# Attention and experts on one core: the tables' writes and constant rows move to ScalarE's queue, and each bf16 part is stored once and repeated by the loads

## The reference

```
q, k, v = split_heads(x @ Wq + bq), split_heads(x @ Wk + bk), split_heads(x @ Wv + bv)
scores = einsum('bhqd,bhkd->bhqk', q, k) / scale
pos_k = (rel_embeddings @ Wk + bk)                      # 128 buckets per head
c2p = take_along_axis(einsum('bhqd,hpd->bhqp', q, pos_k), c2p_pos)
p2c = take_along_axis(einsum('bhkd,hpd->bhkp', k, pos_k), p2c_pos)
scores = scores + (c2p + swapaxes(p2c)) / scale
ctx = einsum('bhqk,bhkd->bhqd', softmax(scores), v)
```

## Time and profile before

| | us |
|---|---|
| median of 3 runs (2073.40 to 2077.61) | 2073.94 |
| the profiled execution | 2074.24 |
| its span, first to last instruction | 2072.4 |
| outside the span | 1.8 |
| PE busy | 1716.4 (83%) |
| DVE busy | 1358.2 (66%) |
| ACT busy | 1071.2 (52%) |
| POOL busy | 1071.1 (52%) |
| DMA moved | 465.95 MB, mean 225 GB/s |
| SP's queue, share of the 16 engines' time | 64.7% |
| ACT's queue, the same | 3.3% |

### The profile page before, as it was taken

How to read it: one execution, slowest core, us unless ns; L and a number is a source line. 1 busy time by engine, 2 the same in 40 slices (tenths; PEclk the granted TensorE clock), 3 DMA queues, 4 the chain that set the end, 5 groups by cost and what they waited for, 6 DMA issues and landing times. The chain is left out here.

```text
span 2072.4 us, 40517 instructions
## 1 busy us (share of the span) xinstructions
PE 1716.4 (83%) x13688; PEld 1153.3 (56%) x13688; DVE 1358.2 (66%) x3937; ACT 1071.2 (52%) x2169; POOL 1071.1 (52%) x1265
## 2 busy tenths in 40 slices
PE   1981159999989899999999999999993566799997
PEld 1440035555555555555555555655552455799996
DVE  1662058789888788888788887888872464243333
ACT  1662136666667566666666666666661461122221
POOL 0210067677766667667576676766740450233332
PEclk9996569999999999999999999999996575899999
DMA  3697378777777877777877777777736961677772
GB/s 117 190 303 245 108 241 265 246 261 251 244 254 257 253 251 245 258 251 259 254 250 257 250 261 248 251 257 254 240 105 154 289 208 36 227 213 221 217 221 81
DMA packets 327354, 465.95 MB, mean 225 GB/s; under 512 B 35516, under 2 KB 260687, under 8 KB 327054
## 3 DMA queue, kind: packets, MB, share of 16 engines
q1 hardware_dynamic: 314814, 428.09, 64.7%
q10 hardware_dynamic: 7344, 20.84, 3.3%
q0 software_dynamic: 4992, 14.43, 1.9%
HBM read 269.90 MB, written 193.65 MB: 224 GB/s over the span
## 5 line engine op out<-in xcount | busy, mean ns | idle before, releaser
L864 ACT ACTIVATE t_probsT<-t_flip 128x512 f32<-128x512 f32 x1024 | 611.5, 607 | 245.2 <-PE t_flip L762 128.0
L816 DVE TENSOR_REDUCE t_most<-t_scores 128x1 f32<-128x640 f32 (+1 forms) x512 | 437.2, 854 | 263.9 <-PE t_scores L739 257.9
L858 ACT COPY t_table<-t_table_ps 128x512 f32<-128x512 f32 x512 | 299.2, 584 | 227.7 <-DMA skew_d<-t_table 138.2
L835 DVE TENSOR_SCALAR t_band<-t_band,t_top 128x384 f32<-128x384 f32 (+1 forms) x512 | 367.6, 718 | 0.0
L912 POOL TENSOR_TENSOR t_near<-t_near,t_masks 128x384 f32<-128x384 f32 (+1 forms) x128 | 147.2, 1150 | 371.6 <-DMA t_near<-skew_d 370.9
L776 PE MATMUL t_sum_ps<-t_probsT,t_vals 128*32 128x256 f32 x4096 | 330.9, 395 | 0.2 <-ACT t_probsT L864 0.2
L718 PE MATMUL t_table_ps<-t_rows,t_quest 96*128 96x256 bf16 x512 | 144.8, 283 | 176.3 <-ACT t_table L858 89.6
L928 POOL TENSOR_TENSOR t_near<-t_near,t_masks 128x768 f32<-128x768 f32 (+1 forms) x128 | 273.1, 2134 | 0.0
L762 PE MATMUL t_flip<-t_masks,t_band 128*128 128x128 f32 x1408 | 262.2, 275 | 0.0
L820 DVE CUSTOM_DVE_ANT_0 t_band<-t_scores,t_near 128x384 f32<-128x384 f32 (+1 forms) x512 | 262.1, 512 | 0.0
L732 PE MATMUL t_scores<-t_after,t_quest 105*128 105x256 bf16 (+3 forms) x1024 | 246.7, 291 | 0.0
(11 more groups left out here) (181 smaller groups left out, 2373.7 us busy)
## 6 DMA issues: line engine op xcount, KB each, us to landing
skew_d<-t_table SPq DMA_DIRECT2D x128, 1024.0 KB, 9.0
t_near<-skew_d SPq DMA_DIRECT2D x128, 640.0 KB, 6.0
t_near<-skew_d SPq DMA_DIRECT2D x128, 384.0 KB, 4.9
e_w<-in_L_ffn_W_dram ACTq DMA_DIRECT2D x39, 512.0 KB, 4.2
e_w<-in_L_ffn_W_dram SPq DMA_DIRECT2D x39, 512.0 KB, 4.0
split_d<-p_part SPq DMA_DIRECT2D x32, 384.0 KB
t_after<-split_d SPq DMA_DIRECT2D x64, 192.0 KB
t_quest<-split_d SPq DMA_DIRECT2D x64, 192.0 KB
```

Source lines behind the costliest of these rows:

```text
L816: nc.vector.tensor_reduce(most[:, c, 1:2], out[:, wide:S], AX.X, ALU.max)
L835: nc.vector.tensor_scalar(band[n % 2][:, t, 0:wide], band[n % 2][:, t, 0:wide], top[n % 2][:, t:t + 1], None, ALU.subtract).then_inc(level ...
L858: nc.scalar.copy(table[:, h, :, u % 4, :], table_ps[:, :, :]).then_inc(table_kept, 1)
L864: nc.scalar.activation(probsT[s % 3][:, half * 512:(half + 1) * 512], flip_ps[half][:, :], ACT.Exp, scale=SCALE).then_inc(expd, 1)
```

## The change

It does four things.

1. `split_d` becomes `[2, N, PARTS, DH, S]`: for each unit and side three parts of 16 rows. `project` stores each part once, again with 12 DMAs a group, each of 128 rows of 1 KB; the DRAM side has levels 8 (heads), 16 (rows), 512 elements, where it was 128 rows outermost.
2. `load_unit` makes the six slots as it loads, with seven DMAs in place of three, in a new order of slots (the slot tables `QSLOTS`, `KSLOTS` and the pick matrices follow it). Six of the seven have an outermost count of 2 on their DRAM side, four of these with a stride of 0 (the repeat). With the far rows there are 10 DMAs a unit (`HATS`), and the same 288 rows of 2 KB land.
3. `skew_write` moves from SP to ScalarE's queue, behind `exponent(back, 1)` of each fourth step.
4. The constant rows (the ones and minus ones) lie next to each other now, so 18 DMAs set them instead of 42. ScalarE issues them at the start of `attend`, from three tiles that DVE and POOL fill. SP begins with `rows`, then unit 0, then `masks`. PE waits for the constants of a buffer when it first scores with it, no longer for all of them at the start.

The core of the diff:

```
-        split_d = dram("split_d", [2, TERMS, N * DH, S], BF16)
+        split_d = dram("split_d", [2, N, PARTS, DH, S], BF16)
...
                     for m in range(4):
-                        for n, (first, step, many) in enumerate((QSLOTS, KSLOTS)[m // 2]):
-                            at = ((m // 2 * TERMS + first) * (N * DH) + b * D + m % 2 * P) * S + half * G
-                            sp.dma_start(view(split_d, at, [[S, P], [step * N * DH * S, many], [1, G]]),
-                                         part[g % 2][:, n, m, :].unsqueeze(1).to_broadcast([P, many, G])
+                        for n in range(PARTS):
+                            slot = QORDER[n] if m // 2 == 0 else n
+                            at = ((m // 2 * N + b * H + m % 2 * 8) * PARTS + slot) * DH * S + half * G
+                            sp.dma_start(view(split_d, at, [[PARTS * DH * S, 8], [S, DH], [1, G]]), part[g % 2][:, n, m, :]
                                          ).then_inc(split_out[g % 2], 16)
...
-                for dst, side_at in ((after[i], TERMS * part), (quest[i], 0), (before[i], TERMS * part)):
-                    sp.dma_start(dst[0:KROWS, :], view(split_d, side_at + n * (DH * S), [[part, TERMS], [S, DH], [1, S]])
-                                 ).then_inc(hats_in[i], 16)
+                block_q, block_k = n * (PARTS * DH * S), (N + n) * (PARTS * DH * S)
+                twice, rows16, rows32 = [[0, 2]], [[S, DH], [1, S]], [[S, 2 * DH], [1, S]]
+                for keys in (after[i], before[i]):
+                    sp.dma_start(keys[0:4 * DH, :], view(split_d, block_k, twice + rows32)).then_inc(hats_in[i], 16)
+                    sp.dma_start(keys[4 * DH:KROWS, :], view(split_d, block_k, [[2 * DH * S, 2]] + rows16)).then_inc(hats_in[i], 16)
+                for slot in (1, 2):
+                    sp.dma_start(quest[i][(slot - 1) * 2 * DH:slot * 2 * DH, :],
+                                 view(split_d, block_q + slot * DH * S, twice + rows16)).then_inc(hats_in[i], 16)
+                sp.dma_start(quest[i][4 * DH:KROWS, :], view(split_d, block_q, rows32)).then_inc(hats_in[i], 16)
...
-            sp.dma_start(masks[:, :, :], c_masks).then_inc(const_in, 16)
-            sp.wait_ge(set_up, 3)
-            for i in range(BUFS):
-                sp.dma_start(quest[i][KROWS + 6:XROWS, :], ones[0:3, :]).then_inc(rows_set, 16)
...
+            sp.dma_start(rows[:, :, :, :].rearrange("p h a v -> p (h a v)"), pick_d[:, :]).then_inc(rows_in, 16)
...
+            def skew_write(n, h):
+                act.wait_ge(table_kept, n * QT + 4 * h + 4)
+                if n >= 2:
+                    act.wait_ge(skew_in[n % 2][0], 16 * 2 * (n // 2))
+                    act.wait_ge(skew_in[n % 2][1], 16 * 2 * (n // 2))
+                nc.scalar.dma_start(view(skew_d, n % 2 * (P * PITCH) + h * 4 * SPOT + 1, [[PITCH, P], [TABLE, 2], [1, 4 * SPOT]]),
+                             table[:, h, :, :, :].rearrange("p a u v -> p a (u v)")).then_inc(skew_out[n % 2][h], 16)
+
+            act.wait_ge(set_up, 4)
+            act.wait_ge(before_set, 3)
+            for i in range(BUFS):
+                for dst, src in ((quest[i][KROWS:FAR, :], ones[0:3, :]), (after[i][FAR:ROWS, :], after_rows[:, :]),
+                                 (before[i][FAR:ROWS, :], before_rows[:, :])):
+                    nc.scalar.dma_start(dst, src).then_inc(rows_set[i], 16)
...
+                if live(s + AHEAD) and s % 4 == 3:
+                    skew_write((s + AHEAD) // QT, s % QT // 4)
```

More of the change, by code:

```diff
@@ L208, in _ @@
             for tab in range(2):
-                for n, (first, step, many) in enumerate((KSLOTS, QSLOTS)[tab]):
-                    for slot in range(first, first + step * many, step):
+                for n, slots in enumerate((KSLOTS, QSLOTS)[tab]):
+                    for slot in slots:
                         for c in range(2):
@@ L559, in attend @@
     BUFS = 6
-    HATS = 6
+    HATS = 10
+    FAR = KROWS + PARTS
     BATCH = H
@@ L581, in attend @@
         ident16 = sb("ident16", [P, P], BF16)
-        ones, minus, zeros = (sb(w, [9, S], BF16) for w in ("ones", "minus", "zeros"))
+        ones, after_rows, before_rows = (sb(w, [9, S], BF16) for w in ("ones", "after_rows", "before_rows"))
         quest, after, before = ([sb(f"{w}{i}", [ROWS, S], BF16) for i in range(BUFS)] for w in ("quest", "after", "before"))
@@ L600, in attend @@
         sum_ps = ps("sum_ps", [P, 512])
-        const_in, rows_in, set_up, rows_set = sem("t_const_in"), sem("t_rows_in"), sem("t_set_up"), sem("t_rows_set")
+        const_in, rows_in, set_up = sem("t_const_in"), sem("t_rows_in"), sem("t_set_up")
+        rows_set = [sem(f"t_rows_set{i}") for i in range(BUFS)]
+        before_set, ident_made = sem("t_before_set"), sem("t_ident_made")
         hats_in = [sem(f"t_hats_in{i}") for i in range(BUFS)]
@@ L626, in _ @@
         def _(sp):
-            part, far = N * DH * S, PARTS * S
+            far = PARTS * S
             def load_unit(n):
@@ L632, in load_unit @@
                     sp.wait_ge(flipped, 2 * QT * (n - BUFS + 1))
-                for dst, side_at in ((after[i], TERMS * part), (quest[i], 0), (before[i], TERMS * part)):
-                    sp.dma_start(dst[0:KROWS, :], view(split_d, side_at + n * (DH * S), [[part, TERMS], [S, DH], [1, S]])
-                                 ).then_inc(hats_in[i], 16)
-                for dst, far_at, many in ((quest[i][KROWS:KROWS + 6, :], n * (2 * far), 2 * PARTS),
-                                          (after[i][KROWS + 6:XROWS, :], (N + n) * (2 * far) + far, PARTS),
-                                          (before[i][KROWS + 6:XROWS, :], (N + n) * (2 * far), PARTS)):
+                block_q, block_k = n * (PARTS * DH * S), (N + n) * (PARTS * DH * S)
[7 more added lines that the diff above has]
+                sp.dma_start(quest[i][4 * DH:KROWS, :], view(split_d, block_q, rows32)).then_inc(hats_in[i], 16)
+                for dst, far_at, many in ((quest[i][FAR:FAR + 6, :], n * (2 * far), 2 * PARTS),
+                                          (after[i][KROWS:FAR, :], (N + n) * (2 * far) + far, PARTS),
+                                          (before[i][KROWS:FAR, :], (N + n) * (2 * far), PARTS)):
                     sp.dma_start(dst, view(far_d, far_at, [[S, many], [1, S]])).then_inc(hats_in[i], 16)
@@ L672, in _ @@
                 sp.sem_clear(semaphore)
-            sp.dma_start(masks[:, :, :], c_masks).then_inc(const_in, 16)
-            sp.wait_ge(set_up, 3)
-            for i in range(BUFS):
-                sp.dma_start(quest[i][KROWS + 6:XROWS, :], ones[0:3, :]).then_inc(rows_set, 16)
-                sp.dma_start(after[i][MROW:ROWS, :], minus[0:3, :]).then_inc(rows_set, 16)
-                sp.dma_start(before[i][MROW:ROWS, :], minus[0:3, :]).then_inc(rows_set, 16)
-                sp.dma_start(after[i][KROWS:KROWS + 3, :], zeros[0:3, :]).then_inc(rows_set, 16)
-                sp.dma_start(after[i][KROWS + 3:KROWS + 6, :], ones[0:3, :]).then_inc(rows_set, 16)
-                sp.dma_start(before[i][KROWS:KROWS + 3, :], ones[0:3, :]).then_inc(rows_set, 16)
-                sp.dma_start(before[i][KROWS + 3:KROWS + 6, :], zeros[0:3, :]).then_inc(rows_set, 16)
+            sp.dma_start(rows[:, :, :, :].rearrange("p h a v -> p (h a v)"), pick_d[:, :]).then_inc(rows_in, 16)
             for u in range(-4, N + 3):
@@ L690, in _ @@
                 if u == -4:
-                    sp.dma_start(rows[:, :, :, :].rearrange("p h a v -> p (h a v)"), pick_d[:, :]).then_inc(rows_in, 16)
+                    sp.dma_start(masks[:, :, :], c_masks).then_inc(const_in, 16)
                 if 0 <= u - 2 < N:
@@ L727, in score @@
                     pe.wait_ge(seen, s - 1)
+                if s == 0:
+                    pe.wait_ge(const_in, 16)
+                    pe.wait_ge(ident_made, 1)
+                if t == 0 and n < BUFS:
+                    pe.wait_ge(rows_set[n], 16 * 3)
                 at = 0
```

33 lines of the change are left out of this document (14 added, 19 removed).

## The result

The changed kernel takes **2216.51 us** (median of 4 runs, 2214.61 to 2217.23) against 2073.67 (2069.92 to 2077.61) for the kernel before beside it: a ratio of 1.0687, 95% interval 1.0672 to 1.0701. The profiled execution has a span of 2214.2 us, 141.8 above the 2072.4 of before.

The account below looks back on a forecast made before the run. Before, PE was nearest to the bound, delayed by the late table write; after, two DMA engines filled by the loads would bound it. 2074.24 - 18 (start) - 5 (projection) + 207 (loads) = 2258 us, range 2110 to 2420.

Parts of the forecast that it names:

- The bound of before: In attend: PE nearest to the bound, held up by the late table write; 19.88 us a unit, 18.20 when nothing stops it.
- The write on ScalarE's queue: In attend: the table's write leaves about 2.3 us earlier; two issues a unit on ScalarE, at most 0.2 us showing each.
- most of the 1.7 us: In attend: what the write's earlier issue would free of the 1.7 us a unit above 18.20.
- The sum: Two engines' time per unit in attend: 10.7 us of loads plus 12.7 us of other traffic, 23.4 us (22.1 to 24.4).
- The loads: Stack loads in attend: outermost count 2 puts 524 kB a unit on two engines, which become the bound; +207 us (+131 to +266).
- the 12.7 us for all other traffic: In attend: 279 kB a unit on each engine besides the loads, at 21.9 GB/s; bounds 11.4 and 13.7 us.
- The start: Start of attend: rows first brings the first score from 70.7 to 53 us into the stage; -18 us (-33 to -5).
- The projection: Last store groups of the projection: stores with half the bytes save 0.7 us a group; -5 us (0 to -16).
- the case: Projection's stores: outermost count 8 means 8 engines, 0.75 us a store against 0.81; the alternative was 16 engines.
- Spread loads: Rival for attend: six or more engines take the loads and the chain is free; 1932 us (1915 to 1960), chance 0.12.
- The clock: Rival for attend: PE waits lower the clock, with three spells 25.7 us a unit; 2394 us or more; above 2420: 0.05.
- The signs: Profile after: period 22 to 25 us, some 18 after unit 60; share under 0.75, lone 0.12 to 0.15; first table 15 to 20 us.

Follow-up runs that it names:

- e2: The kernel before with only the tables' writes moved from SP's to ScalarE's queue: 1981.9 us, ratio 0.9579.
- e7: e1 with split_d laid out as part, row, column, stores with 128 rows outermost, nine loads of 32 rows with 16 outermost: 1919.2 us, ratio 0.9281.
- e9: e1 with its seven stack loads made nine of 32 rows each, stores and layout kept: 1925.6 us, ratio 0.9324.
- e6: The changed kernel with only the tables' writes put back into SP's queue: 2443.4 us, ratio 1.1831.
- e3: The kernel before with its three stack loads cut into nine of 32 rows, two slots outermost, writes left on SP: 2516.8 us, ratio 1.2164.
- e1: The changed kernel with 16 or 32 rows outermost in its stack loads and the repeat or slots inside: 1959.6 us, ratio 0.9462.
- e10: The changed kernel with only the query's repeated loads spread (four of 16 rows, 16 outermost), keys left at 2: 2069.4 us, ratio 1.0016.
- e8: The kernel before with only the new start (rows first, constants on ScalarE's queue): 2042.6 us, ratio 0.9880.

## Why the prediction was right, step by step

The forecast was 2258 us in a range of 2110 to 2420, slower with a chance of 0.84; it came to 2216.5.

- **The bound of before** held. e2 takes the late write away and leaves 18.52 us a unit; the shortest possible was read as 18.20, and e7 and e9 have means of 18.29 and 18.21.
- **The write on ScalarE's queue.** Right: "most of the 1.7 us" was 1.36 us a unit in e2. Its issues cost 0.53 us in the median (L880: 520 to 631 ns) and show little: e2's unit is only 0.3 us above 18.20. What the step left out: the first units gain too (unit 0's copy comes 10.7 us sooner in e2), and beside two-engine loads the move is worth 227 us, not nothing. The sum let the two engines decide "whatever the queue's order gains". With the write on SP (e6) they did not decide alone; the queue's order did, at 26.3. The sum has no term for that order: it would give e6 the same 23.4 us a unit, and it gave e3 200 us too little. That it came out for the changed kernel rests on the write's move in the same change.
- **The loads**, the main term: the mechanism is shown (share 0.13, never fewer than two packets in flight; e1, e10). The size was 22.59 us a unit where the sum had 23.4, so +162.8 us over 60 periods and not +207 over 59. The mis-sized part is the 12.7 us for all other traffic on an engine: 22.59 - 10.7 leaves 11.9, nearer to the lower bound (11.4 at 24.4 GB/s) than to the middle that I took. With only two engines crowded, their traffic seems to run at the rate of the lone loads: 262 kB of two-engine loads and 283 kB of the rest in 22.59 us are 24.1 GB/s an engine (the trace does not say which engine moved a packet, so this is an estimate). The dose e10 then fell where that rate puts it, 20.2.
- **The start** was -18 and came to far less. To unit 0's copy, by which the account above goes, it is -7.6. The step itself went by the first score (70.7 us into the stage, to come down to 53) and by the read of `near` for which it waits. The first score with `near` came 71.5 us into the stage before (272.50) and comes after 67.2 now (257.29). That is -4.4, just outside the bounds of -33 and -5. The rows after, SP's queue, PE and GpSimd:

```profile
213.53 0.37 PE L707 MATMUL t_table_ps<-t_rows,t_quest 96*128 96x256 bf16 x1 [52.35 <-DMA t_before<-far_d]
...
236.09 9.40 SPq L664 DMA_DIRECT2D t_near<-skew_d  x4
...
251.77 0.99 POOL L922 TENSOR_TENSOR t_near<-t_near,t_masks 128x384 f32<-128x384 f32 x1 [27.78 <-DMA t_near<-skew_d]
...
257.29 0.69 PE L733 MATMUL t_scores<-t_masks,t_near 128*128 128x128 f32 x2 [7.96 <-POOLq L941]
```

  The first read of `near` was issued 46 us into the stage, where the step had 43. But it landed 15.7 us later, in place of 5: it shares the two engines with three units' loads. And the first table came after 23.4 us, not 15 to 20: it waits for the last load of unit 0 (`t_before<-far_d`) and not for `rows`, which no longer comes last. The step read the wait of before and did not ask what would be late next. The same score before:

```profile
272.50 0.63 PE L739 MATMUL t_scores<-t_masks,t_near 128*128 128x128 f32 x2
```

- **The projection** was -5 with bounds 0 and -16; it gave -10.8. The count of 8 does hold the stores (e7: -17.3 with 128). The Trainium skill (DMA: Bandwidth & Descriptors, "Why a DMA increments its semaphore by 16 and not by 1") gives 8 engines for 128 rows against 8; the share of 0.52 agrees. So the case was picked rightly, but its price was low: 11.6 us a group (162.43 to 174.06) against 13.07 before, so 1.4 us saved in each late group where the working had 0.7.
- **The rivals.** Spread loads would give 1932 in my working; e1 has 1960, e9 1926. The clock did fall (0.93 in the middle), but PE was busy 86% of that stretch, so PE at a lower clock was not the bound.
- **The signs**: period 22.59, then 17.7, 16.4, 15.1; share 0.69; lone share 0.13 at 46 to 54 GB/s; GpSimd's and PE's waits; held issues; ScalarE's wait gone. Only the first table missed, 23.4 us into the stage where 15 to 20 was said.

Against the measurement the sum was 44 us too high in the loads, 6 too high in the projection and 2.5 in what follows unit 60, and 10 too low in the start. Together that is 42, the distance from 2258 to the profiled 2215.9. The start's miss hid a quarter of the loads'.

## What to carry to other kernels

Look at the outermost level of both sides of every DMA: if it is small, put a level of 16, 32 or 128 there (the counts run here) and the repeat or the slot inside; here that order alone was worth 257 us, with the same bytes. Judge a transfer by what its busiest engine carries (its own share plus a sixteenth of all other traffic), not by the mean DMA share, which fell here while the kernel became DMA-bound. And a write on which a chain rests does not belong in the queue of bulk loads, where both its issue and the next read wait.

The best kernel of this study is e7: the change as it is, with 16 rows outermost in the loads and 128 in the stores, 1919.2 us, 7.2% under the kernel before.

## What the runs showed of the hardware that I had not expected

- Two engines filled by loads slow what stands behind the loads in the same queue: reads of `near` landed in 11.8 and 9.7 us in the median, where e1 has 6.1 and 6.3, though the other fourteen engines had room. The write in ScalarE's queue was hardly slowed: 8.2 us, with 7.5 in e1 and 8.3 in e2, where the loads have six engines.
- Two-engine loads cost 3.7 us a unit with the write in another queue (22.59 against e1's 18.92) and 6.4 with it in the same (e6's 26.30 against the 19.89 of e8, whose loads are on six engines): a queue's order adds to what a slow transfer costs.
- Two 64-row loads with 32 outermost are worse than four of 32 rows with 16 outermost, at the same bytes: 1959.6 us against 1925.6, 18.92 against 18.21 us a unit in the profiles. The cause stays open.
- 128 rows instead of 8 outermost brought twelve stores of 128 KB from 8.8 to 6.6 us of issue time and the DMA share beside them from 0.52 to 0.97; `attend` began 8.4 us sooner than in e1.
